# Four-layer gated cross-attention on one core: another order of the first loads, of the weight preparation and of VectorE's small work

## The chip, the cores and the metric

The kernel runs on one core of a Trainium2 chip. The metric is the device time of one execution in microseconds (us), the median of several runs. Everything is computed in float32. TensorE (PE) multiplies matrices, VectorE (DVE), ScalarE (ACT) and GpSimd (POOL) do the rest, and SyncE (SP) issues all transfers. A high-precision product is made from two parts of each operand, a rounded high part (ACT writes it) and the low part that is left (POOL or DVE subtracts), in three passes: high x high, high x low, low x high.

## What is computed

```python
# x, ctx: 8 blocks of 128 rows x 512.  LN = layer norm, g = gates
x = x + tanh(g_xattn[0]) * xattn0(LN(x), ctx)  # 32 heads of 128, position bias, mask; own residual
x = x + tanh(g_ffn[0])   * ffn0(LN(x))         # base + top-2 of 8 rank-16 experts
x = x + tanh(g_xattn[1]) * xattn1(LN(x), ctx)  # 16 query heads on 4 key heads of 96
x = x + tanh(g_ffn[1])   * ffn1(LN(x))         # as ffn0
x = x + tanh(g_xattn[2]) * xattn2(LN(x), ctx)  # one head of 512: softmax((x Wq+bq)(ctx Wk+bk)^T) ctx
x = x + tanh(g_ffn[2])   * ffn2(LN(x))         # w = (q - zero_point) * scale, by groups; x w^T + bias
x = x + tanh(g_xattn[3]) * xattn3(LN(x), ctx)  # 32 query heads of 16 on 8 key heads
x = x + tanh(g_ffn[3])   * ffn3(LN(x))         # activations rounded to -127..127 per row, gate/up/down
```

## The kernel before

Each engine has its own program, written out by hand in the order in which it shall run; semaphores join them. Rows go in blocks of 128 tokens, and from the second half-layer on in 4 pairs of blocks (`NPAIR`), inside which `j` is 0 or 1. `i` is the pair, `u` one of 8 units of a pair in the last attention.

**Prelude (first some 60 us).** SP issues the keys' weights of the first head pair (first chunk, then the rest), the transposed context in 4 chunks `c`, x in two halves of 4 blocks, the values' weights, the queries' weights and small tables (L388 to L404), all in one queue. ACT rounds chunk by chunk, DVE writes the context's low parts (L1737), POOL those of the weights (L526, L531). PE warms up with `BUSY` small products of the identity (L1122), then makes 4 key units chunk by chunk (L1131), and 8 value units (L1117). Between value units 1 to 5 it turns the blocks k and k+4 of x (`turn_x(k)`, L1145: a product with a diagonal matrix that also scales). For that DVE computes statistics of all 8 blocks (L1743 to L1754), POOL the powers (L537, L539), DVE applies them to 8 blocks (L1757), sums the query weights' blocks (`weight_sums`) and, for each k, multiplies what was turned by `ln_w` and forms sums (`rows_sums(k)`, L1766 to L1775) and later their low parts (`rows_low(k)`, L1780). `turn_x(k+1)` waits until `rows_sums(k)` has read the bank. POOL writes the low part of the first query weights (`split("q", 0)`, L520). The first query unit (L1098) waits for `x_split` and `wq_lo`.

**The head-pair loop** follows (some 80 to 810 us), then ffn0, xattn1 and ffn1. The change does not touch them.

**xattn2 (some 1304 to 1378 us).** Per pair PE runs `x2_pe(i)`: turn the next pair's rows (L1302), scores (L1485), first half of the next pair's keys (L1322), transpose the probabilities (L1493), second half of the keys, output (L1499), the next queries (L1322). DVE's `x2_dve(i)` takes row maxima (L2114), divides (L2118), writes low parts, statistics and keys, and updates x. Ahead of the first pair DVE dequantises ffn2's weights: 4 subtractions (L2371) and 4 multiplications (L2374) over 128x512 each. ACT rounds the result (`f2_weights`, before pair 2), POOL subtracts (L579). POOL also writes the context's low parts for the next pair (`context_rest`, L579), which the keys wait for (`cT_lo`).

**xattn3 (some 1408 to 1581 us)** works unit by unit: scores for unit U+2 (L1552), transposes of unit U (L1559), a filler product, then `attend(U)` (L1574). DVE's unit takes maxima and reciprocals and, after them, a slice of ffn3's preparation for the pair before (`first_pair`, `middle_pair`, `last_pair`): scales (L2143), rounding (`f3_round`, L2165), clipping (`f3_clip`, L2171). POOL divides the probabilities (L660) and multiplies (L652).

**ffn3 (the last 50 us)** per pair i: `f3_turn(i+1)`, `f3_gate_up(i+1, 0)`, transposes of pair i's inner rows (L1670), `f3_gate_up(i+1, 1)` (L1662), `f3_down(i)` (L1679). Before the very last transposes PE runs `BUSY_END` products of the identity (L1717).

## Time and profile before

| | |
|---|---|
| median of 3 runs | 1632.13 us (1632.02 to 1634.69) |
| profiled execution | 1633.68 us, its span 1632.0 us |
| TensorE clock granted, mean | 0.993 |
| busy: PE, DVE, ACT, POOL | 97%, 61%, 45%, 25% |
| PE not busy | 53.2 us of the span |

A busy share is an average over stages; the stages have different limits. Line numbers (L1131) are those of the kernel before. In a timeline, a row merges neighbouring instructions of one line: start, time from the first start to the last end, engine, line, what is written and read, how many, and in brackets the idle time of that engine ahead of it with what ended it.

### The profile page before, as it was taken

The numbers are of one execution on the slowest core, as the hardware profiler recorded it, in microseconds if no ns is written. First come the engines' busy times: TensorE is split into PE (matmuls) and PEld (weight loads), VectorE is DVE, ScalarE is ACT, GpSimd is POOL, SyncE is SP. The second block draws the span as 40 slices with busy tenths as digits, with TensorE's granted clock in tenths as the row PEclk, the third lists the DMA queues.
The fourth block names the chain that finished last, engine by engine and source line by source line (L and its number), as shares of the span: only waits on it lengthen the run. The fifth ranks groups of instructions, "written<-read, shape, count | busy, mean of one in ns | idle before, by whom it ended". The sixth has DMA issues, their size and how long they took to land.

```text
span 1632.0 us, 25948 instructions
## 1 busy us (share of the span) xinstructions
PE 1578.8 (97%) x8970; PEld 1267.8 (78%) x8970; DVE 989.5 (61%) x2627; ACT 741.7 (45%) x2149; POOL 403.5 (25%) x279
## 2 busy tenths in 40 slices
PE   8999999999999999999989999999999999899987
PEld 6788888888888888888875878778686787665556
DVE  6762663626636356363776674848475766756677
ACT  4442443424434244343432562726354322388863
POOL 3131320313203132031213300000001433376650
PEclk9999999999999999999999999999999999999999
DMA  5110111101111011110234000000001613000001
GB/s 177 53 43 30 56 42 51 42 29 55 42 51 42 29 55 42 51 42 29 78 88 184 14 1 13 0 13 0 0 1 41 219 52 106 14 14 14 1 1 52
DMA packets 34404, 76.22 MB, mean 47 GB/s; under 512 B 5537, under 2 KB 18465, under 8 KB 32161
## 3 DMA queue, kind: packets, MB, share of 16 engines
q1 hardware_dynamic: 34336, 75.36, 13.9%
q8 instruction: 38, 0.62, 0.2%
q14 instruction: 30, 0.24, 0.1%
HBM read 73.25 MB, written 2.10 MB: 46 GB/s over the span
## 4 chain that ended last, share of the span: by engine, by line
PE 79%; DVE 10%; ACT 5%; issue 3%; DVEq 2%; POOL 1%; DMA 1%; SPq 0%; POOLq 0%; ACTq 0%
PE banks L1172 11%; PE banks L1117 10%; PE banks L1090 9%; PE banks L1098 9%; PE banks L1322 9%; PE banks L1426 5%; PE banks L1228 3%; PE banks L1211 3%; PE banks L1398 3%; PE banks L1218 2%; PE banks L1529 2%; ACT p L967 1%; PE banks L1536 1%; PE banks L1552 1%; PE banks L1346 1%
## 5 line engine op out<-in xcount | busy, mean ns | idle before, releaser
L520 POOL TENSOR_TENSOR w_q<-w_raw_q,w_q 128x1792 fp32r<-128x1792 f32 x16 | 65.3, 4082 | 485.2 <-ACT w_q L727 485.2
L1172 PE MATMUL banks<-w_o,atT 128*128 128x512 f32 x720 | 180.2, 396 | 0.0
L1090 PE MATMUL banks<-cT,w_k 128*128 128x512 f32 x720 | 178.0, 396 | 0.0
L1117 PE MATMUL banks<-w_v,cT 128*128 128x512 f32 x768 | 177.3, 390 | 0.6 <-POOL w_v L531 0.4
L1117 PEld LDWEIGHTS banks<-w_v,cT 128*128 128x128 f32 x768 | 143.6, 188 | 31.6 <-POOL w_v L531 1.3
L1098 PE MATMUL banks<-xT,w_q 128*128 128x512 f32 x672 | 163.7, 394 | 0.7 <-ACT kT L717 0.7
L1841 DVE TENSOR_TENSOR sA<-banks,pbias 128x512 f32<-128x512 f32 x64 | 44.1, 690 | 186.4 <-PE banks L1211 185.7
L1172 PEld LDWEIGHTS banks<-w_o,atT 128*128 128x128 f32 x720 | 131.9, 188 | 25.7
L1090 PEld LDWEIGHTS banks<-cT,w_k 128*128 128x128 f32 x720 | 131.9, 188 | 25.6
L1098 PEld LDWEIGHTS banks<-xT,w_q 128*128 128x128 f32 x672 | 123.7, 188 | 26.0 <-ACT kT L717 1.1
L781 ACT ACTIVATE sA<-sA,nmA 128x128 f32<-128x128 f32 x256 | 99.5, 393 | 57.0 <-DVE nmA L1846 56.7
L1322 PE MATMUL banks<-xnT_part,wq 128*128 128x256 f32 x768 | 101.3, 285 | 0.0
L1868 DVE TENSOR_TENSOR x_res<-banks,x_res 128x512 f32<-128x512 f32 x112 | 77.1, 689 | 35.8 <-PE banks L1172 34.7
L717 ACT ACTIVATE vA<-banks 128x512 f32<-128x512 f32 x64 | 38.2, 597 | 131.0 <-PE banks L1117 130.9
L1322 PEld LDWEIGHTS banks<-xnT_part,wq 128*128 128x128 f32 x768 | 94.1, 190 | 2.2 <-issue 2.2
L967 ACT ACTIVATE p<-banks,nm 128x128 f32<-128x128 f32 x256 | 91.4, 407 | 8.7 <-DVE nm L2192 8.6
L891 ACT ACTIVATE p<-banks,nm 128x256 f32<-128x256 f32 x128 | 58.7, 484 | 68.0 <-DVE nm L2059 68.0
L787 ACT ACTIVATE pTA<-banks 128x512 f32<-128x512 f32 x64 | 38.1, 595 | 108.5 <-PE banks L1218 108.5
L1426 PE MATMUL banks<-wo,at 128*128 128x512 f32 x192 | 85.7, 592 | 0.0
L791 ACT ACTIVATE atT<-banks 128x512 fp32r<-128x512 f32 x64 | 38.3, 599 | 98.9 <-PE banks L1228 98.9
L1846 DVE CUSTOM_DVE_ANT_0 sA<-sA,madd 128x128 f32<-128x128 f32 x256 | 77.3, 357 | 8.8 <-issue 0.5
L660 POOL TENSOR_TENSOR p<-p,rs 128x512 f32<-128x512 f32 x64 | 67.9, 1066 | 41.3 <-DVE rs L2198 40.7
(280 smaller groups left out, 3246.4 us busy)
## 6 DMA issues: line engine op xcount, KB each, us to landing
w_raw_v<-in_w0v SPq DMA_DIRECT2D x8, 1024.0 KB, 4.8
w_raw_q<-in_w0q SPq DMA_DIRECT2D x16, 512.0 KB, 3.4
w_raw_k<-in_w0k SPq DMA_DIRECT2D x15, 512.0 KB, 3.5
w_raw_o<-in_w0o SPq DMA_DIRECT2D x15, 512.0 KB, 3.3
cTp<-in_ctxT SPq DMA_DIRECT2D x12, 512.0 KB, 3.9
wq_raw<-in_wq SPq DMA_DIRECT2D x1, 3072.0 KB, 10.2
wo<-in_wo SPq DMA_DIRECT2D x1, 3072.0 KB, 19.9
x_res<-in_x SPq DMA_DIRECT2D x2, 1024.0 KB, 10.9
```

What stands on the lines that cost most here:

```text
L520: pool.tensor_tensor(w_part[slot][1][:], w_raw[slot][:], w_part[slot][0][:].bitcast(F32), ALU.subtract).then_inc(S(f"w{slot}_lo"), 1)
L660: pool.tensor_tensor(p3[:, U % 3, k], p3[:, U % 3, k], rs[:, U % 3, k].unsqueeze(2).to_broadcast([P, 4, P]), ALU.mult).then_inc(S(f"x3_p{h ...
L781: e = act.activation(sA[:, g % 2, t, :], sA[:, g % 2, t, :], ACT.Exp, bias=nmA[:, g % 2, t:t + 1], scale=-1.0, accum_out=smA[:, g % 2, t:t ...
L967: e = act.activation(p3[:, U % 3, n, :], s[:, k, :], ACT.Exp, bias=nm[:, U % 3, n:n + 1], accum_out=sm[:, U % 3, n:n + 1])
L1090: mm = pe.matmul(dst, wk_[l][:, c, h * P:(h + 1) * P], cT[r][:, c, half * HT:(half + 1) * HT], start=c == 0 and n == 0, stop=c == DC - 1 a ...
L1098: mm = pe.matmul(dst, wq_[l][:, w, c, :], xT[r][:, x, c, :], start=c == 0 and n == 0, stop=c == 1 and n == len(PASSES) - 1)
L1117: mm = pe.matmul(dst, cT[l][:, c, b * P:(b + 1) * P], wv_[r][:, c, :], start=n == 0, stop=n == 3 * DC - 1)
L1172: mm = pe.matmul(dst, atT[l][:, h, t], w[r][:, h, :], start=n == 0, stop=n == 5)
L1322: mm = pe.matmul(dst, w(l, c), x(r, c), start=c == 0 and n == 0, stop=c == DC - 1 and n == len(PASSES) - 1)
L1426: mm = pe.matmul(bank(6 + b), at1[:, n, b * P:(b + 1) * P], wo1[:, n, :], start=n == 0, stop=n == NCH * KV1 - 1)
L1846: e = dve.tensor_tensor_reduce(out=sA[:, h, t, :], in0=sA[:, h, t, :], in1=madd[:, 4 * half + t, :], scale=-1.0, scalar=0.1 * BIG, op0=ALU ...
L1868: dve.tensor_tensor(x_res[:, b, :], bank(6 + b % 2), x_res[:, b, :], ALU.add).then_inc(S("o_added"), 1)
```

## The change

It reorders the first loads and cuts context chunk 1 in two for the rounding; it works the statistics by halves of 4 blocks; it moves the low part of the first query weights from POOL to DVE; it puts the dequantising for ffn2 between the pairs of xattn2, splits the keys there 3 to 1 around the transposes, moves one query product of xattn3 ahead of the first scores, moves slices of ffn3's preparation between units, moves one gate/up product ahead of a wait, and halves the last identity products. The rest of the arithmetic is as before.

```diff
-BUSY_END = 12
+BUSY_END = 6
-K_PARTS = (slice(0, 2 * P), slice(2 * P, DC * 2 * P))
+K_PARTS = (slice(0, 2 * P), slice(2 * P, 4 * P), slice(4 * P, DC * 2 * P))
+C_PARTS = [(c, slice(h * HT, (h + 1) * HT)) for c in range(2) for h in range(2)] + [(c, slice(0, NB * P)) for c in (2, 3)]
+X_ORDER = [b for k in range(NPAIR) for b in (k, k + NPAIR)]
...
# SyncE
-            sp.dma_start(w_raw["k"][:, K_PARTS[1]], A["w0k"][0][:, K_PARTS[1]]).then_inc(S("wk_ld"), 16)
-            for c in range(1, DC):
+            sp.dma_start(c_raw[:, 1, :], A["ctxT"][:, 1, :]).then_inc(S("c1_loaded"), 16)
+            k_rest = slice(K_PARTS[1].start, K_PARTS[2].stop)
+            sp.dma_start(w_raw["k"][:, k_rest], A["w0k"][0][:, k_rest]).then_inc(S("wk_ld"), 16)
+            for c in range(2, DC):
                 sp.dma_start(c_raw[:, c, :], A["ctxT"][:, c, :]).then_inc(S(f"c{c}_loaded"), 16)
-            for k in range(2):
-                sp.dma_start(x_res[:, 4 * k:4 * k + 4, :], x_dram[:, 4 * k:4 * k + 4, :]).then_inc(S(f"x{k}_loaded"), 16)
             load("v", A["w0v"][0])
+            for n in range(2):
+                for b in (2 * n, NPAIR + 2 * n):
+                    sp.dma_start(x_res[:, b:b + 2, :], x_dram[:, b:b + 2, :]).then_inc(S(f"x{n}_loaded"), 16)
             load("q", A["w0q"][0])
...
# GpSimd
-            pool.wait_ge(S("a_var"), 1)
-            pool.tensor_tensor(rstd[:], ve[:], neg_half[:], ALU.pow).then_inc(S("a_rstd"), 1)
-            pool.wait_ge(S("a_var"), 2)
-            pool.tensor_tensor(rr[:], ms[:], neg_half[:], ALU.pow).then_inc(S("a_rstd"), 1)
-            pool.wait_ge(S("xr_ready"), NB)
-            split("q", 0)
+            for n in range(2):
+                t = slice(n * NPAIR, (n + 1) * NPAIR)
+                pool.wait_ge(S("a_var"), n + 1)
+                pool.tensor_tensor(xrs[:, :, t], xvar[:, :, t], neg_half[:, 0:NPAIR].unsqueeze(1).to_broadcast([P, 2, NPAIR]),
+                                   ALU.pow).then_inc(S("a_rstd"), 1)
             split("k", 1)
...
# ScalarE: context by C_PARTS, the keys' weights in three parts
+            store_v(0, bank(0), K_UNITS + 1)
             act.wait_ge(S("const_ready"), 1)
-            act.wait_ge(S("a_rstd"), 2)
-            diagonal(0)
-            store_v(0, bank(0), K_UNITS + 1)
-            for k in range(1, NPAIR):
+            for k in range(NPAIR):
+                if k % 2 == 0:
+                    act.wait_ge(S("a_rstd"), k // 2 + 1)
                 diagonal(k)
-            store_v(1, bank(1), K_UNITS + 2)
-            round_q(0)
+                if k == 1:
+                    store_v(1, bank(1), K_UNITS + 2)
             for b in range(2, NB):
                 store_v(b, bank(b % 2), K_UNITS + b + 1)
                 if b < 2 + NPAIR:
                     rows_high(b - 2)
+                if b == 2:
+                    round_q(0)
...
# TensorE
-                pe.wait_ge(S("c_lo"), c + 2 if c else 1)
-                for n, u in enumerate((0, 2, 1, 3) if c == 0 else range(4)):
+                pe.wait_ge(S("c_lo"), 2 * c + 1 if c < 2 else c + 3)
+                for n, u in enumerate((0, 2, 1, 3) if c < 2 else range(4)):
...
                 if not last:
-                    x2_keys(i + 1, 0)
+                    x2_keys(i + 1, range(DC - 1))
                 for j in range(2):
                     pe.wait_ge(S("x2_p"), 2 * i + j + 1)
                     pe.transpose(bank(2 + j)[:, 0:P], p2[:, j, :], ident[:]).then_inc(S("x2_tp"), 1)
                 if not last:
-                    x2_keys(i + 1, 1)
+                    x2_keys(i + 1, (DC - 1,))
...
                 pe.wait_ge(S("kv3_ready"), 4)
+                x3_queries(0, 2, 3, 6)
                 scores(0)
                 scores(1)
-                x3_queries(0, 2, G3, 6)
+                x3_queries(0, 3, G3, 6)
...
                 f3_gate_up(i + 1, 0)
+                if i == 0:
+                    f3_gate_up(i + 1, 1)
                 f3_turn_inner(i, 0)
                 f3_turn_inner(i, 1)
-                f3_gate_up(i + 1, 1)
+                if i > 0:
+                    f3_gate_up(i + 1, 1)
...
# VectorE, first layer (the statistics, their scales and their use are now
# functions of a half n; x_stats, x_scales and x_apply each take 4 blocks)
+            x_stats(0)
+            x_scales(0)
+            x_stats(1)
+            x_apply(0)
+            x_scales(1)
             dve.wait_ge(S("g_loaded"), 64)
...
-            for k in range(NPAIR):
-                rows_sums(k)
-                if k >= 1:
-                    rows_low(k - 1)
+            rows_sums(0)
+            x_apply(1)
+            weight_sums(0)
+            rows_sums(1)
+            rows_low(0)
+            dve.wait_ge(S("wq_hi"), 1)
+            dve.tensor_tensor(w_part["q"][1][:], w_raw["q"][:], w_part["q"][0][:].bitcast(F32),
+                              ALU.subtract).then_inc(S("wq_lo"), 1)
+            rows_sums(2)
+            rows_low(1)
+            rows_sums(3)
+            rows_low(2)
             rows_low(NPAIR - 1, 0, 0, 2)
             rows_low(NPAIR - 1, 1, 2, 7)
...
# VectorE, fourth layer, middle_pair
+                    if u == 2 and i + 2 < NPAIR:
+                        ln_stats(2 * i + 4)
                     if u == 2 and i > 1:
                         f3_scales(i - 2)
                         f3_round(i - 2)
                     if u == 3:
                         f3_apply(i - 1)
-                        if i + 2 < NPAIR:
-                            ln_stats(2 * i + 4)
# last_pair
                     if u == 0:
                         f3_max(i - 2, 1, 1)
+                        f3_scales(i - 2)
                     if u == 1:
                         updated(i - 1, 1)
-                        f3_scales(i - 2)
+                        f3_round(i - 2, (0,))
                     if u == 2:
                         ln_stats(2 * i - 2, 2, "f3_var")
-                        f3_round(i - 2)
                     if u == 3:
+                        f3_round(i - 2, (1,))
                         f3_apply(i - 1)
-                    if u == 4:
-                        f3_clip(i - 2)
...
                 updated(NPAIR - 1, 0)
-                f3_clip(NPAIR - 2)
+                f3_clip(NPAIR - 3)
                 updated(NPAIR - 1, 1)
...
             ln_stats(NB - 2, 2, "f3_var")
+            f3_clip(NPAIR - 2, (0,))
             f3_apply(NPAIR - 1)
...
             inner_clip()
+            f3_clip(NPAIR - 2, (1,))
             f3_max(NPAIR - 1, 0, 1)
...
# VectorE, third layer (layer index 2)
-            dve.wait_ge(S("f2_ld"), 16 * (1 + 4 * DC))
-            for c in range(DC):
-                dve.tensor_tensor(zp2[:, c, :], w2q[:, c, :], zp2[:, c, :], ALU.subtract)
-            dve.drain()
-            for c in range(DC):
-                dve.tensor_tensor(zp2[:, c, :], zp2[:, c, :], sc2[:, c, :], ALU.mult)
-            dve.drain().then_inc(S("scaled"), 1)
+            (the same two loops are now f2_offsets() and f2_scales())
             next_stats(0)
             next_apply(L2X, 0)
             x2_keys(0)
-            pairs_split(dve, x2_dve, nothing, nothing, nothing)
+            x2_dve(0, False)
+            f2_offsets()
+            x2_dve(1, False)
+            f2_scales()
+            x2_dve(2, False)
+            x2_dve(3, True)
```

## Rows read from the trace of the kernel before

**Rows 1.** The page's busy times.

```profile
PE 1578.8 (97%) x8970; PEld 1267.8 (78%) x8970; DVE 989.5 (61%) x2627; ACT 741.7 (45%) x2149; POOL 403.5 (25%) x279
```

**Rows 2.** PE's waits over the span: us in total, times, longest.

```profile
PE banks L1670 <- DVE iq L2348: 6.3, 4, 3.2
```

**Rows 3.** Timeline, start and arrival of loads (start, us, engine, line).

```profile
11.75 10.04 PE L1131 MATMUL banks<-cT,w_k 128*128 128x512 f32 x36 [2.12 <-DVE cT L1737]
...
14.06 2.47 DVE L1743 BATCH_NORM_STATS2 stat<-x_res 128x6 f32<-128x512 f32 x4 [0.18 <-DMA x_res<-in_x]
...
19.25 2.19 ACT L713 ACTIVATE w_v<-w_raw_v 128x512 fp32r<-128x512 f32 x4 [6.84 <-DMA w_raw_v<-in_w0v]
```

**Rows 4.** Timeline, the rows of x in the prelude.

```profile
29.07 2.05 PE L1145 MATMUL banks<-diag,x_res 128*128 128x128 f32 x16 [0.31 <-ACT diag L757]
...
33.95 4.22 POOL L520 TENSOR_TENSOR w_q<-w_raw_q,w_q 128x1792 fp32r<-128x1792 f32 x1 [5.73 <-ACT w_q L727]
34.20 4.25 DVE L1773 TENSOR_TENSOR stage_q<-stage_q 128x256 f32<-128x256 f32 x1
...
47.34 2.02 DVE L1780 TENSOR_TENSOR xT<-stage_o,xT 128x1792 fp32r<-128x1792 f32 x1
...
55.18 5.18 PE L1098 MATMUL banks<-xT,w_q 128*128 128x512 f32 x22
```

**Rows 5.** Busy times by window; behind POOL's the granted clock.

```profile
14.00:16.00 2.00, 2.00 (x6) 1.54 (x5) 1.94 (x4) 0.00 (x0) 0.00 (x0) 0.50 1.09 410
...
1322.00:1324.00 2.00, 2.00 (x10) 2.00 (x11) 0.00 (x0) 0.00 (x0) 0.00 (x0) 0.50 0.49 133
```

**Rows 6.** Timeline, start of xattn2; last row: the second pair's keys.

```profile
1306.39 6.48 DVE L2371 TENSOR_TENSOR zp<-w2q,zp 128x512 f32<-128x512 int32 x4
...
1318.17 3.14 POOL L579 TENSOR_TENSOR cT_part<-cTp,cT_part 128x256 fp32r<-128x256 f32 x4
...
1319.23 0.66 PE L1302 MATMUL banks<-ident,xn 128*128 128x128 f32 x4 [2.68 <-DVE xn L1829]
...
1321.84 3.78 PE L1485 MATMUL banks<-k,q 128*128 128x128 f32 x16 [0.63 <-DVE k L2108]
1325.27 3.72 PE L1322 MATMUL banks<-cT_part,wk 128*128 128x256 f32 x24
...
1341.63 3.08 PE L1322 MATMUL banks<-cT_part,wk 128*128 128x256 f32 x24
```

**Rows 7.** Timeline, xattn2's later pairs.

```profile
1339.93 1.95 PE L1485 MATMUL banks<-k,q 128*128 128x128 f32 x16
...
1341.47 0.29 DVE L2114 TENSOR_REDUCE nm<-banks 128x1 f32<-128x128 f32 x1 [5.85 <-PE banks L1485]
...
1361.59 0.33 PE L1493 MATMUL banks<-ident,p 128*128 128x128 f32 x1 [0.89 <-DVE p L2118]
```

**Rows 8.** Timeline, PE in xattn3: first scores, and keys in pair 1.

```profile
1416.55 1.99 PE L1552 MATMUL banks<-kbd,q 64*128 64x512 f32 x8 [1.08 <-ACT q L958]
...
1487.04 1.99 PE L1514 MATMUL banks<-cTp,wk 128*128 128x256 f32 x8 [1.20 <-DVE y L2202]
```

**Rows 9.** Timeline, last pair of xattn3.

```profile
1559.64 2.45 DVE L2165 TENSOR_SCALAR qs<-xs,rsc 128x512 f32<-128x512 f32 x4
...
1568.37 4.10 DVE L2171 TENSOR_SCALAR qs<-qs 128x512 f32<-128x512 f32 x4
...
1574.33 0.65 PE L1559 MATMUL banks<-ident,p 128*128 128x128 f32 x4 [1.09 <-POOL p L660]
```

**Rows 10.** Timeline, ffn3.

```profile
1596.58 1.12 PE L1670 MATMUL banks<-ident,iq 128*128 128x128 f32 x4 [3.21 <-DVE iq L2348]
1597.35 3.28 PE L1662 MATMUL banks<-wg,qTs 128*128 128x256 f32 x16
...
1601.17 0.48 DVE L2329 SCALAR_TENSOR_TENSOR sg<-banks,xsc,eg 128x256 f32<-128x256 f32 x1 [1.51 <-ACT eg L1007]
...
1623.86 2.84 PE L1717 MATMUL banks<-ident 128*128 128x128 f32 x24
```

More of the change, by code:

```diff
@@ L185, in build @@
         rv = sb(ctx_a, "rv", [P, NB])
[L186 to L187 removed]
+        xvar = sb(ctx_a, "xvar", [P, 2, NB])
+        xrs = sb(ctx_a, "xrs", [P, 2, NB])
         ctx_a.close()
@@ L732, in _ @@
                 context_chunk(0, slice(half * HT, (half + 1) * HT), "ab"[half])
+            for c, t in C_PARTS[2:4]:
+                context_chunk(c, t)
             act.wait_ge(S("wk_ld"), 16)
             round_part("k", K_PARTS[1])
-            for c in range(1, DC):
-                context_chunk(c)
+            round_part("k", K_PARTS[2])
+            for c, t in C_PARTS[4:]:
+                context_chunk(c, t)
             act.wait_ge(S("wv_ld"), 16)
@@ L1460, in x1_pe, with x2_product @@
                 project(1, NCH * (KV1 - 1), NCH * KV1)
-            def x2_product(w, t, b0, done, halves=(0, 1)):
-                for oc in range(DC // 2 * halves[0], DC // 2 * (halves[-1] + 1)):
+            def x2_product(w, t, b0, done, chunks=range(DC)):
+                for oc in chunks:
                     mm = split_product(bank(b0 + oc // 2)[:, (oc % 2) * PT2:(oc % 2 + 1) * PT2],
@@ L1691, in _ @@
             pe.wait_ge(S("res"), NB * L2X)
-            x2_keys(0, 0)
-            x2_keys(0, 1)
+            x2_keys(0, range(DC))
             pairs_ahead(pe, x2_pe)
@@ L1733, in weight_sums @@
                 dve.tensor_tensor(w[:, WS4], w[:, W12], w[:, WS2], ALU.subtract).then_inc(S("q_sum"), 1)
-            for n, (c, t) in enumerate([(0, slice(0, HT)), (0, slice(HT, NB * P))] + [(c, slice(0, NB * P)) for c in range(1, DC)]):
+            for n, (c, t) in enumerate(C_PARTS):
                 dve.wait_ge(S("c_hi"), n + 1)
@@ L1759, in _, with x_stats, x_scales @@
-            weight_sums(0)
+            def x_stats(n):
+                dve.wait_ge(S(f"x{n}_loaded"), 32)
+                for k in range(n * NPAIR, (n + 1) * NPAIR):
+                    dve.bn_stats(stat[:, k, :], x_res[:, X_ORDER[k], :])
+            def x_scales(n):
+                t = slice(n * NPAIR, (n + 1) * NPAIR)
+                dve.drain()
+                for k in range(n * NPAIR, (n + 1) * NPAIR):
+                    dve.bn_aggr(mv[:, k, :], stat[:, k, :])
+                dve.drain()
+                dve.tensor_scalar(xvar[:, 0, t], mv[:, t, 1], EPS, None, ALU.add)
+                dve.drain()
+                dve.reciprocal(rv[:, t], xvar[:, 0, t])
+                dve.drain()
+                dve.tensor_tensor(xvar[:, 1, t], mv[:, t, 1], rv[:, t], ALU.mult)
+                dve.drain()
+                dve.tensor_scalar(xvar[:, 1, t], xvar[:, 1, t], EPS, None, ALU.add).then_inc(S("a_var"), 1)
@@ L1760, in _, with x_apply @@
+            def x_apply(n):
+                dve.wait_ge(S("a_rstd"), n + 1)
+                for k in range(n * NPAIR, (n + 1) * NPAIR):
+                    b = X_ORDER[k]
+                    dve.tensor_scalar(x_res[:, b, :], x_res[:, b, :], mv[:, k, 0:1], xrs[:, 0, k:k + 1], ALU.subtract,
+                                      ALU.mult).then_inc(S("xr_ready"), 1)
+            x_stats(0)
[3 more added lines that the diff above has]
+            x_scales(1)
             dve.wait_ge(S("g_loaded"), 64)
@@ L2160, in f3_scales, with f3_round @@
                 scales(xsc[:, i], rsc[:], am[:])
-            def f3_round(i):
-                for j in range(2):
+            def f3_round(i, js=(0, 1)):
+                for j in js:
                     for w in range(2):
```

46 lines of the change are left out of this document (17 added, 29 removed).

## The prediction, made before the changed kernel was run

> **What bounds the kernel now.** I read the page's busy times first: PE is busy for 1578.8 us of the 1632.0 us span, so all its waiting is 53.2 us [rows 1]. Then PE's waits, first in total and then stretch by stretch. The head-pair loop (80 to 800 us) shows none, the change does not touch it, and ffn0, xattn1 and ffn1 keep theirs. So the sum is made of waits at four places: the prelude, the start of xattn2, xattn3 and ffn3, where the largest wait sits (L1670, 6.3 us in 4 times) [rows 2]. Third the windows with the granted clock. Some waits are followed by PE at half clock (0.50, the level of 1.2 GHz) [rows 5]: such a wait costs twice, once as idle time and once in slower matmuls.
>
> **Prelude.** PE waits 2.12 us for context chunk 1 at 11.75, then the 36 matmuls take 10.04 us, with the clock at 0.50 from 14 to 16 [rows 3, 5]. At full clock a value unit's 12 matmuls follow each other every 2.8 us, so the 36 would take 8.4. Now chunk 1 comes before the rest of the keys' weights and is split by halves. DVE can finish it by 9.8 and POOL its weights by 10.2, so PE would begin some 1.5 us earlier and, if the clock stays up, end its keys 3.2 us earlier, at 18.6. The values' weights no longer wait behind x. x's first megabyte is usable at 14.06 and the values' weights, the second megabyte after it, at 19.25 [rows 3]: 2.6 us each. So the weights arrive at about 14.1, x's halves at 16.7 and 19.2, and both value units can be done at 24.1. After that the chain is DVE's. From the rows: statistics of 4 blocks take 2.47 [rows 3], and I take 1.4 for scales, 1.7 for POOL's power, 1.9 to apply 4 blocks, 3.1 for a `rows_sums`, 1.8 for the weight sums and 2.02 for a low part of 128x1792 [rows 4]. In the new order that makes statistics to 19.3, scales to 21.0 (POOL is still on the values), statistics to 23.5, apply to 25.4. The first turn of x is then at 24.5, against 29.07 [rows 4].
>
> From there PE has 24 us of work up to the queries, but DVE has more. The query weights' low part moves onto it (+2.0). What goes is a stall: POOL's 4.22 us at 33.95 covers DVE's L1773, which takes 4.25 us for 128x256 [rows 4], where its neighbours take 0.43, so 3.8 us come back. Adding the list up, the sums of k=2 come at 41.2, the last turn waits about 2.3 us for them, and DVE gives the first queries' rows free at 51.4 with PE done at 51.8. Queries began at 55.18 [rows 4]: 3.4 us. That new wait may bring a short half clock, worth up to 1.7. I take 3.0; bounds 0 (DVE eats it all) and 5.
>
> The Trainium skill (SBUF — State Buffer, Who interferes with whom) says that VectorE and GpSimd take a shared port pair in turns, and that the second to come stands still for the whole of the other's instruction. The L1773 row agrees. By it a DVE instruction moved into a time when POOL works can cost POOL's length. The place to fear it here is the dequantising, the second rival.
>
> **Start of xattn2.** DVE's subtractions take 6.48 us and push the turned rows back: PE waits 2.68 us before L1302 at 1319.23, then 0.63, and then runs the scores in 3.78 us instead of 1.95, at clock 0.50 [rows 5 to 7]. With both dequantising steps gone from there, the statistics run at 1306.4, and the rows are ready near 1312.3, after POOL's low parts. PE finishes the first keys at 1316.55 and turns x at once. DVE's last two key copies (0.8) let the scores start at 1317.65, not 1321.84. But a wait takes part of the place. The next keys need the context's low part, for which ACT copies only after 1316.55 (1.1 us) and POOL takes 3.1 [rows 6]: 1320.8. The scores end at 1319.4, so PE waits about 1.4 us that was hidden before. The keys start at 1320.8 instead of 1325.27 [rows 6], 4.5 us, and their 24 matmuls take the 3.08 of later pairs, not 3.72 [rows 6]: 5.1 in all. Bounds: 3 (the clock falls again) and 6.8 (no such wait).
>
> The subtractions now stand behind pair 0's updates, the multiplications behind pair 1's. In each pair DVE has an empty 5.85 us there [rows 7]. Free of POOL the steps take 0.68 and 0.62 us an instruction, 2.7 and 2.5 in all. POOL's context parts may cost 1.3 more, so each fits, and nothing is added. ACT's rounding before pair 2 finds its input a microsecond or so early.
>
> **Keys 3 to 1.** At pair 2 ACT and POOL prepare ffn2's weights, the probabilities come late, and PE waits 0.89 for the second block and 0.18 before the first [rows 7]. One key chunk is worth 1.46 us, so the longer cover hides both: 1.1 us. After the transposes 1.46 us of keys remain, more than the 0.9 that ACT's copies need. In pairs 0 and 1 nothing waited, so nothing changes.
>
> **xattn3.** The query product moved ahead (1.8 us) fills the 1.08 us wait [rows 8] but starts the scores 0.6 us later. ACT and not PE then sets the pace, and it gets its second queries 0.3 us earlier: 0.3 (0 to 1.1). In pair 1 PE waits 1.20 us for the copy of y [rows 8], and straight ahead of the copy stand 1.7 us of statistics. A unit earlier they delay a row maximum by 0.5 that has 0.9 to spare: 1.2. In the last pair the 2.45 us of rounding is split in two and the 4.10 us of clipping leaves the loop [rows 9]. After the clipping PE waited 1.09 for POOL [rows 9] and 0.70 for ACT. The maximum behind it can come 2.7 us earlier, but ACT's copies and POOL's queue give back only 1.0 to 1.5. The half of the rounding before the copy of y eats what the other half saves there, so the 1.38 us wait and the half clock near 1566 stay. I take 1.3 (0.5 to 4, the upper end if that wait and its half clock go too).
>
> **ffn3.** The 3.21 us wait [rows 10] takes in the gate/up product, 2.15 us of PE at full clock, which took 3.28 after it. But DVE's chain sets the end. It can use an earlier sigmoid: at 1601.17 it had waited 1.51 [rows 10]. Against that it now carries half a clipping (0.7) there, so 0.8. The other half falls into 0.82 us in which DVE waited for POOL's power. At the end the 12 identity products take 2.84 us from 1623.86 and reach 1626.4 [rows 10], while the inner rows were ready at 1625.5. Half of them, 1.4 us, ends before that: 0.9.
>
> **Sum.** 3.0 + 5.1 + 1.1 + 0.3 + 1.2 + 1.3 + 0.8 + 0.9 = 13.7 us. The profiled execution took 1633.68 us, 1.55 more than the median, and would come to 1620.0; from the median 1632.13 it is **1618.4 us**. With every part at its lower end 7.5 us remain, 1624.6; with every part at its upper end it is 20.9, 1611.2.
>
> **Rivals.**
> *The prelude gives nothing* (0.15). Moving the low part makes DVE the bound of the rows of x. For it: DVE is at work almost without a break from 27 to 56 us. Against: the 3.8 us stall goes for 2.0 us of work. Time: 1632.1 - 10.7 = 1621.4.
> *The dequantising collides with POOL in the attention* (0.04), the case on the other side. The four subtractions took 6.48 us beside POOL [rows 6]; three of them ran in 0.6, so one stood for some 4.6. If all eight instructions did, a group would take 18.5 us in a gap of 5.85 [rows 7]: 12.7 late, twice, with some 2.4 at half clock after each. Time: 1632.1 - 13.7 + 25.4 + 4.8 = 1648.6. It decides from the point where a group takes more than the gap and has eaten the 13.7, that is from about 11 us a group. Against it: POOL has one block of 3.1 us there [rows 6], not a row of them.
> *More than I see comes back* (0.17). The clock stays up through the last pair and the last turn of x, and the context's low part is in time: 6 us more, 1612.5.
> *The waits go but others fill in* (0.06), because DVE is in every chain: only xattn2's statistics and the identity products count, 1626.
> *The forecast itself* has 0.58.
>
> **How the numbers follow.** The likeliest case gives 1618.4. The range 1612.5 to 1624.0 takes in the first and most of the third rival and leaves out some 0.15. What a measurement can tell from no change is 0.2%, 3.3 us. Faster by more is all but the second rival and the tail of the fourth: 0.93; within it 0.03; slower 0.04.
>
> **What would show it.** Prelude: L1131's second group starts near 10.2 and its clock stays up; queries start near 52; the L1773 row is 0.43; the last turn of x waits 2 us. xattn2: no wait of L1302, a new wait of L1322 for POOL's context part of about 1.4, L2371 about 2.7 to 4 after the first pair. xattn3: no wait for y in pair 1; no L2171 inside the last pair. ffn3: the first L1670 wait about 1.1 and the last row of identity products half as long. A span above 1625, or the queries after 54, would prove me wrong in the prelude; keys of pair 1 after 1322, counted with the prelude's shift, in xattn2.

## The result, and the profile after

| | before | after |
|---|---|---|
| median, runs of the first comparison | 1632.86 us (4 runs, 1632.02 to 1634.69) | 1619.04 us (4 runs, 1618.59 to 1620.08) |
| ratio, 95% interval | | 0.9915 (0.9898 to 0.9932) |
| median, second comparison | 1631.89 us (11 runs, 1629.27 to 1637.60) | 1618.80 us (5 runs, 1617.55 to 1622.02) |
| ratio, 95% interval | | 0.9918 (0.9901 to 0.9935) |
| profiled execution, its span | 1633.68, 1632.0 us | 1619.05, 1617.3 us |

The change takes 13.1 to 13.8 us off the median; 13.7 were forecast from the profiled execution. The two profiled spans differ by 14.7 us. The rows of after, one fence for each view, with the group of before that each answers to. The page's busy times [rows 1] and PE's waits in total [rows 2]:

```profile
PE 1572.8 (97%) x8958; PEld 1264.1 (78%) x8958; DVE 981.2 (61%) x2633; ACT 742.1 (46%) x2151; POOL 399.3 (25%) x278
...
PE banks L1682 <- DVE iq L2380: 4.8, 4, 1.6
```

The prelude of after, timeline [rows 3, 4]:

```profile
7.33 11.49 PE L1142 MATMUL banks<-cT,w_k 128*128 128x512 f32 x48
...
14.02 2.20 ACT L719 ACTIVATE w_v<-w_raw_v 128x512 fp32r<-128x512 f32 x4 [1.47 <-DMA w_raw_v<-in_w0v]
...
16.74 2.47 DVE L1757 BATCH_NORM_STATS2 stat<-x_res 128x6 f32<-128x512 f32 x4 [2.84 <-DMA x_res<-in_x]
...
24.09 1.95 PE L1156 MATMUL banks<-diag,x_res 128*128 128x128 f32 x16
...
35.02 0.42 DVE L1798 TENSOR_TENSOR stage_o<-stage_o 128x256 f32<-128x256 f32 x1
...
37.79 2.02 DVE L1814 TENSOR_TENSOR w_q<-w_raw_q,w_q 128x1792 fp32r<-128x1792 f32 x1
...
40.55 2.02 PE L1156 MATMUL banks<-diag,x_res 128*128 128x128 f32 x16 [2.17 <-DVE stage_a L1791]
```

All 48 key products run without a wait; the small instruction that took 4.25 us takes 0.42; the last turn of x waits 2.17 us (2.3 forecast). The queries begin at 50.61, against 55.18. Then xattn2, timeline [rows 6, 7]:

```profile
1314.11 2.05 PE L1496 MATMUL banks<-k,q 128*128 128x128 f32 x16 [0.27 <-DVE k L2141]
...
1316.97 4.35 PE L1333 MATMUL banks<-cT_part,wk 128*128 128x256 f32 x36 [0.81 <-POOL cT_part L585]
...
1322.76 1.88 PE L1510 MATMUL banks<-ctk,pT 128*128 128x512 f32 x4
...
1326.42 3.02 DVE L2404 TENSOR_TENSOR zp<-w2q,zp 128x512 f32<-128x512 int32 x4
1332.54 0.29 DVE L2147 TENSOR_REDUCE nm<-banks 128x1 f32<-128x128 f32 x1 [3.10 <-PE banks L1496]
...
1352.95 0.38 PE L1504 MATMUL banks<-ident,p 128*128 128x128 f32 x2
```

PE's wait for the turned rows is gone, there is a new one of 0.81 for the context's low part (1.4 forecast), four subtractions in 3.02 us with 3.10 idle behind them, and no wait for probabilities at pair 2. xattn3 and ffn3, timeline of PE [rows 8 to 10]:

```profile
1413.05 1.13 PE L1563 MATMUL banks<-kbd,q 64*128 64x512 f32 x4 [1.66 <-ACT q L969]
...
1553.59 1.48 PE L1540 MATMUL banks<-wo,y 128*128 128x512 f32 x2 [1.53 <-DVE y L2235]
...
1562.97 0.91 PE L1585 MATMUL banks<-pT,vbd 128*32 128x128 f32 x16 [0.70 <-ACT pT L985]
...
1577.78 4.06 PE L1674 MATMUL banks<-wg,qTs 128*128 128x256 f32 x32 [0.55 <-DVE sg L2365]
1583.16 0.66 PE L1682 MATMUL banks<-ident,iq 128*128 128x128 f32 x4 [1.32 <-DVE iq L2380]
```

Windows with the granted clock behind POOL's busy time [rows 5]:

```profile
14.00:16.00 2.00, 2.00 (x11) 1.65 (x10) 0.00 (x0) 1.98 (x4) 1.27 (x2) 1.00 1.05 397
...
1322.00:1324.00 2.00, 2.00 (x12) 1.33 (x11) 1.04 (x3) 0.96 (x1) 0.00 (x0) 1.00 0.00 0
1554.00:1556.00 2.00, 2.00 (x18) 0.60 (x16) 0.97 (x4) 1.83 (x11) 2.00 (x2) 0.56 0.00 0
...
1586.00:1588.00 2.00, 2.00 (x8) 1.60 (x8) 1.66 (x6) 1.45 (x3) 0.00 (x0) 0.50 0.00 0
```

The half clock is gone at 14 and at 1322. In this execution it stays behind the wait for y, and in ffn3 it has moved to the product behind the transposes. One more difference was in no step of the forecast: in ffn1's last pair, whose code is unchanged, PE of after waited 1.21 us for `hs` (the experts' inner rows, which VectorE writes and PE transposes) and PE of before did not. So one question of the experiments was how much of a pair of profiles holds for the runs.

### The profile page after: what moved, and what is told of

Its sections match the earlier page's. It is cut to its first block, busy times and chain, and to the rows that moved or that the text cites. A ratio compares the mean times of both kernels' runs of the same rounds, so it can differ in the third digit from the quotient of the medians.

```text
span 1617.3 us, 25912 instructions
## 1 busy us (share of the span) xinstructions
PE 1572.8 (97%) x8958; PEld 1264.1 (78%) x8958; DVE 981.2 (61%) x2633; ACT 742.1 (46%) x2151; POOL 399.3 (25%) x278
## 4 chain that ended last, share of the span: by engine, by line
PE 78%; DVE 10%; ACT 5%; issue 3%; DVEq 2%; POOL 1%; DMA 1%; POOLq 0%; SPq 0%; ACTq 0%
PE banks L1183 11%; PE banks L1128 10%; PE banks L1101 9%; PE banks L1109 9%; PE banks L1333 9%; PE banks L1437 5%; PE banks L1239 4%; PE banks L1222 3%; PE banks L1409 3%; ACT p L978 2%; PE banks L1229 2%; PE banks L1540 2%; PE banks L1563 1%; PE banks L1357 1%; PE banks L1547 1%
## 5 line engine op out<-in xcount | busy, mean ns | idle before, releaser
L527 POOL TENSOR_TENSOR w_q<-w_raw_q,w_q 128x1792 fp32r<-128x1792 f32 x15 | 61.1, 4070 | 479.6 <-ACT w_q L733 479.6
L585 POOL TENSOR_TENSOR cT_part<-cTp,cT_part 128x256 fp32r<-128x256 f32 x32 | 23.3, 765 | 228.5 <-ACT cT_part L858 228.5
```

The costliest lines, as they stand in the source:

```text
L527: pool.tensor_tensor(w_part[slot][1][:], w_raw[slot][:], w_part[slot][0][:].bitcast(F32), ALU.subtract).then_inc(S(f"w{slot}_lo"), 1)
```

## The experiments

Twelve further sets of runs followed, in three groups of four; each group shares its runs of before (medians 1632.46, 1631.89 and 1631.43 us). Each kernel left one profile.

### The parts, each alone on the kernel before

**Prelude alone** (`a1_prelude`): all edits of the change up to the head-pair loop.

```diff
+ C_PARTS, K_PARTS in three, loads in the new order, x_stats/x_scales/x_apply by halves
-            split("q", 0)                      # GpSimd
+            dve.tensor_tensor(w_part["q"][1][:], w_raw["q"][:], ...)   # VectorE, behind rows_low(0)
```

> The kernel before with the prelude's part of the change alone (order of the loads, context chunk 1 by halves, statistics by halves, the first query weights' low part on VectorE). Theory from the two traces: the first queries start 4.6 us earlier than before, near 50.6, and this carries through the untouched middle; the time falls by 4.6 us, or by 3.4 if the one small VectorE instruction in ffn1's last pair (L1855 after the change, 1.67 us instead of 0.38) again stands for a whole POOL instruction. The forecast said 3.0. Rival, the prelude gives nothing because VectorE becomes the bound: within 1 us of before. If the ffn1 stall is chance, this profile or one of the next three lacks it; if it hangs on the prelude's shift, it is here and in none of the runs without the prelude.

Measured: 1628.85 us (11 runs, 1627.24 to 1633.18), ratio 0.9980 (0.9971 to 0.9989), 3.6 us less by medians. But its profiled execution was a long one (1631.15), and its queries started at 54.61, only 0.6 earlier. Its timeline of PE, the products of chunk 1 and the last turn of x:

```profile
11.87 10.07 PE L1142 MATMUL banks<-cT,w_k 128*128 128x512 f32 x36 [1.83 <-POOL w_k L533]
...
42.92 3.55 PE L1156 MATMUL banks<-diag,x_res 128*128 128x128 f32 x16 [1.92 <-DVE stage_a L1788]
```

The first load landed 0.55 us later than in after (ACT rounds it at 3.78, not 3.23), context chunk 1 was rounded at 9.28 and not 7.73, so PE waited 1.83, and the clock stood at 0.61 and 0.54 from 12 to 16. The `hs` wait was there as well (1.22). The 4.0 us between this start of the queries and after's are, by the rows, three parts: x's first half was usable 1.31 us later (VectorE's statistics start at 18.05, not 16.74), PE's late keys held up VectorE's sums by 1.05, and the last turn was followed by half clock, 1.6 more (`c_loads`, below). The gain is real and varies. The rival that the `hs` wait hangs on the prelude falls with `a3_x3` and `a4_end`, which have the wait without this prelude.

**Dequantising alone** (`a2_dequant`).

```diff
-            (subtractions and multiplications)   next_stats(0) ... pairs_split(dve, x2_dve, ...)
+            x2_dve(0, False); f2_offsets(); x2_dve(1, False); f2_scales(); x2_dve(2, False); x2_dve(3, True)
```

> The kernel before with only the dequantising moved into xattn2's attention. Theory: the second keys start some 5 us earlier although nothing else has changed, and the 5.85 us gaps of VectorE hide the two steps (about 3.0 us each): time lower by 5.1 to 5.7 us. Rival, collision with POOL in the gaps: a step takes over 5 us and the gain falls under 3 us. Rival, the gain needs the three to one split of the keys: the waits for the probabilities at pair 2 grow and under 4 us remain.

Measured: 1629.76 us (11 runs, 1628.58 to 1631.62), ratio 0.9985 (0.9976 to 0.9994), 2.7 us less by medians: a miss, although its profile shows the whole 5.5 us in its place (output of pair 0 at 1326.33, against 1331.88) and neither rival: the two groups took 3.02 and 2.95 us, and only 0.4 us was lost from there to xattn3's keys. The next two profiles suggest a reason.

**xattn3's part alone** (`a3_x3`).

```diff
+                x3_queries(0, 2, 3, 6)      # ahead of scores(0), scores(1)
+                    ln_stats(2 * i + 4) in unit 2; last pair: scales in unit 0, rounding in units 1 and 3, no clipping
```

> The kernel before with only xattn3's part: one query product ahead of the first scores, and VectorE's statistics, rounding and clipping moved between units. The forecast's terms give 0.3 + 1.2 + 1.3 = 2.8 us less; by the two traces it is 0.4 + 1.15 + 2.4 = 4.0 us less. Rival, the moved clipping comes back at the start of ffn3 (its half there is paid for in full): under 2 us less.

Measured: 1627.62 us (6 runs, 1626.97 to 1628.10), ratio 0.9966 (0.9954 to 0.9978), 4.8 us less by medians; the rival falls. From xattn3's first keys to the last down product it took 216.0 us, against 219.5 in before: 3.5. Its course through the untouched ffn1 and xattn2 differs from the profile of before, though (timeline, all engines):

```profile
1297.44 1.65 DVE L1823 TENSOR_SCALAR ve<-mv 128x2 f32<-128x2 f32 x1
...
1302.43 0.53 PE L1349 MATMUL banks<-ident,hs 128*128 128x128 f32 x2 [1.20 <-DVE hs L2007]
...
1307.29 5.29 DVE L2371 TENSOR_TENSOR zp<-w2q,zp 128x512 f32<-128x512 int32 x4
1308.55 4.62 POOL L579 TENSOR_TENSOR cT_part<-cTp,cT_part 128x256 fp32r<-128x256 f32 x4
...
1321.12 2.05 PE L1485 MATMUL banks<-k,q 128*128 128x128 f32 x16 [1.03 <-DVE k L2109]
```

A VectorE instruction on two numbers per row takes 1.65 us, PE waits 1.20 for `hs`; then VectorE's subtractions take 5.29 and not 6.48 us, GpSimd's context part stands still instead (4.62, not 2.86), and the scores run in 2.05, not in 3.78 at half clock.

**ffn3's part alone** (`a4_end`).

```diff
+                if i == 0: f3_gate_up(i + 1, 1)      # ahead of the transposes
-BUSY_END = 12
+BUSY_END = 6
```

> The kernel before with only ffn3's part: the second gate/up product of pair 1 ahead of pair 0's transposes, and 6 identity products at the end instead of 12. Forecast 0.8 + 0.9 = 1.7 us less, by the two traces about 1.5 us less. Rival, the half clock only moves from the gate/up product to the product behind it and VectorE's chain sets the end: 0.9 us less, the identity products alone.

Measured: 1630.28 us (11 runs, 1628.65 to 1630.88), ratio 0.9984 (0.9975 to 0.9993), 2.2 us less; by its profile 2.6 us from xattn3's first keys on. The second transposes of inner rows follow the first after 8.98 us:

```profile
1595.07 0.66 PE L1670 MATMUL banks<-ident,iq 128*128 128x128 f32 x4 [1.32 <-DVE iq L2351]
...
1604.05 0.66 PE L1670 MATMUL banks<-ident,iq 128*128 128x128 f32 x4 [1.13 <-DVE iq L2351]
```

In before it was 10.59 (10.10 to 11.07 in the three other profiles with ffn3 as in before), in after 10.33. So the gate/up product is worth more by itself (1.6 us) than in the whole change, where VectorE carries a clipping in that stretch.

### On the changed kernel

**The changed kernel again** (`b0_after`), no edit.

> The changed kernel itself, once more, beside more runs of before. The four single parts summed to 13.3 us of medians without the keys' split. Theory: 13.3 + 1.1 for the keys, less some 1.3 that ffn3 gives back when the clipping stands in VectorE's chain there, so about 13 us under before. Two places of a profile should differ from execution to execution: the prelude (the second group of key products either follows without a wait at full clock and the queries start near 50.6, or the first loads land about 1.3 us later, PE waits some 1.8 us and runs at half clock, and the queries start up to 4 us later), and ffn1's last pair (a 1.2 us wait for hs, or none). Rival: those two are fixed properties of the changed kernel, and this profile repeats the first one in both.

Measured: see the table on top; 13.1 us under before, as expected. In its profile chunk 1's products waited 0.85 us, the queries started at 51.76, and the `hs` wait was there (1.21). The first place varies as expected; the second showed the `hs` wait in every profile with this prelude, and only `c_poolq` (below), which changes the prelude, lacks it.

**Keys 2 to 2 again** (`b1_keys22`).

```diff
-                    x2_keys(i + 1, range(DC - 1))
+                    x2_keys(i + 1, range(DC // 2))
```

> The changed kernel with xattn2's keys split 2 to 2 around the transposes again. Theory: PE waits 0.9 us for the second block's probabilities at pair 2 and 0.2 before the first, output of pair 2 comes 1.1 to 1.2 us later, and the time is 1.1 us above the changed kernel. Rival, the three to one split costs each pair something (pairs took 15.91 us after and 15.72 in the profile of before): the loop's period falls to 15.72 and only 0.7 us are lost. Against it: with the dequantising alone moved, at 2 to 2, the period was 15.92 too.

Measured: 1621.39 us (6 runs, 1618.88 to 1624.09), ratio 0.9931 (0.9915 to 0.9947), 2.6 us above the changed kernel by medians, an interval that holds 0 and the 1.1. The profile gives the size: the wait is back,

```profile
1354.52 0.33 PE L1504 MATMUL banks<-ident,p 128*128 128x128 f32 x1 [0.89 <-DVE p L2151]
```

and from pair 0's output to xattn3's keys it takes 76.66 us, against 74.93 to 75.49 in the seven profiles at 3 to 1: 1.2 to 1.7. The wait itself is worth 1.2: from pair 1's output to pair 2's it takes 17.09 us, against 15.91 in after. The rival falls: the first period is 15.92 and did not shrink.

**Clipping beside the wait** (`b2_clip`).

```diff
                 f3_clip(NPAIR - 3)
+                f3_clip(NPAIR - 2)
                 updated(NPAIR - 1, 1)
...
-            f3_clip(NPAIR - 2, (0,))   # and (1,), both in ffn3
```

> The changed kernel with pair 2's clipping taken out of VectorE's chain in ffn3 and put where VectorE waits 1.90 us for the last but one output of xattn3, as in the kernel before, behind pair 1's clipping. Theory: ffn3's second transposes of inner rows follow the first after 9.0 us, as they did with ffn3's part alone, and not after 10.3; the 0.7 before the first are saved too: 1.3 to 2.0 us under the changed kernel. Rival, a half clock in ffn3 or ScalarE sets the end there: under 0.5 us.

Measured: 1617.97 us (4 runs, 1616.74 to 1619.43), ratio 0.9912 (0.9893 to 0.9931); 0.8 us under the changed kernel, not settled by these runs. The profile shows the step at 9.34 us, not 9.0:

```profile
1582.51 0.66 PE L1682 MATMUL banks<-ident,iq 128*128 128x128 f32 x4 [1.33 <-DVE iq L2381]
...
1591.85 0.66 PE L1682 MATMUL banks<-ident,iq 128*128 128x128 f32 x4 [1.48 <-DVE iq L2381]
```

From xattn3's keys to the end 1.1 us are saved (212.1, against 213.2 in `b0_after`), a little under the 1.3 expected.

**And the last pair's rounding behind y** (`b3_clip_last`), on top of `b2_clip`.

```diff
                     if u == 3:
-                        f3_round(i - 2, (1,)); f3_apply(i - 1)
+                        f3_apply(i - 1, (0,))
+                    if u == 4:
+                        f3_round(i - 2, (1,)); f3_apply(i - 1, (1,))
```

> As the one before, and in the last pair of xattn3 the second half of the rounding and of the normalisation stand behind the copy of y, a unit later. Theory: y is copied 1.7 us earlier, PE's 1.53 us wait for it goes, and the half clock that follows (1554 to 1558) goes with it: 1.5 to 3 us more. Rival, the moved instructions meet GpSimd's row of multiplications in that unit and stand for them, the row maxima come late: nothing gained, or up to 2 us lost, to be seen as long instances of the rounding or the normalisation.

Measured: 1617.28 us (4 runs, 1615.10 to 1618.93), ratio 0.9902 (0.9883 to 0.9922). The stage from xattn3's keys to the end is 212.07 us, as without it (212.11): nothing gained, as the rival had it. Timeline of PE:

```profile
1554.20 1.12 PE L1540 MATMUL banks<-wo,y 128*128 128x512 f32 x2 [0.23 <-DVE y L2235]
...
1558.14 0.66 PE L1570 MATMUL banks<-ident,p 128*128 128x128 f32 x4 [0.52 <-POOL p L666]
...
1561.12 0.66 PE L1570 MATMUL banks<-ident,p 128*128 128x128 f32 x4 [0.90 <-POOL p L666]
1562.12 0.66 PE L1570 MATMUL banks<-ident,p 128*128 128x128 f32 x4 [0.34 <-POOL p L666]
```

1.30 us of the wait for y go. In their place stand 2.1 us of waits for GpSimd's divisions (the three shown and one more of 0.34), where `b2_clip` has 0.53, and two roundings took 1.87 us where they had taken 1.22. `b2_clip` had no half clock behind its wait for y, so this pair does not test whether the half clock goes with the wait.

**Chunk 1's weights first** (`c_loads`).

```diff
+            sp.dma_start(w_raw["k"][:, K_PARTS[1]], ...)   # 128 KB, then the context chunk
             sp.dma_start(c_raw[:, 1, :], ...)
-            sp.dma_start(w_raw["k"][:, k_rest], ...)       # 384 KB
+            sp.dma_start(w_raw["k"][:, K_PARTS[2]], ...)   # 256 KB
```

> The changed kernel with the keys' weights for chunk 1 (128 KB) loaded and rounded ahead of context chunk 1, and the weights of chunks 2 and 3 (256 KB) behind it, instead of all 384 KB behind it. In four of five profiles since, PE waited 0.8 to 1.8 us before chunk 1's products, each time for the low part of these weights, and the queries started at 51.2 to 54.6 instead of 50.6. Theory: that wait goes in this profile, the queries start at 50.5 to 51.5, and the median is 1 to 2 us under the changed kernel. Rival, the context chunk's own low part becomes the last: a wait of about 0.5 stays and the gain is under 0.5 us.

Measured: 1619.92 us (5 runs, 1617.66 to 1621.09), ratio 0.9923 (0.9910 to 0.9936): nothing gained (the changed kernel had 0.9918). The wait at chunk 1 is gone in its profile, and the queries still start at 52.55. One part of the cause is when x lands (timeline of DVE, then of PE):

```profile
17.05 2.47 DVE L1758 BATCH_NORM_STATS2 stat<-x_res 128x6 f32<-128x512 f32 x4 [2.92 <-DMA x_res<-in_x]
...
40.87 2.83 PE L1157 MATMUL banks<-diag,x_res 128*128 128x128 f32 x16 [2.14 <-DVE stage_a L1792]
```

The last turn starts 23.82 us after VectorE's first statistics. In after, `b0_after`, `b1_keys22`, `b2_clip`, `b3_clip_last` and `c_best` it is 23.81 to 23.83, with x usable anywhere from 16.74 to 17.89. The other part stands behind the last turn, in the granted clock of this window, of this kernel:

```profile
42.00:44.00 2.00, 2.00 (x11) 1.90 (x10) 1.93 (x4) 0.79 (x1) 0.00 (x0) 0.50 0.03 8
```

and of the profiled execution of after:

```profile
42.00:44.00 2.00, 2.00 (x13) 1.74 (x12) 1.93 (x4) 1.10 (x1) 0.00 (x0) 1.00 0.04 8
```

In seven profiles with this wait at 2.13 to 2.17 us the queries start 10.04 to 10.06 us after the last turn (four) or 11.66 to 11.68 after it (three, each with the half clock). `a1_prelude`, with a wait of 1.92, took 11.69. So x's landing and the chain of VectorE behind it set that turn, and not the wait at chunk 1, as long as that is short; in `a1_prelude`, where it was 1.83 with half clock behind it, PE came late to the first turn and the last one stood 24.87 us after the first statistics.

**Low part on GpSimd again** (`c_poolq`).

```diff
+            split("q", 0)     # GpSimd, behind its second power
-            dve.tensor_tensor(w_part["q"][1][:], ...)
```

> The changed kernel with the low part of the first query weights on GpSimd again. Theory: one small instruction of VectorE (128x256, 0.42 us) stands for GpSimd's 4.2 us again, the sums of k=1 or k=2 come some 2 us later net (3.8 more, 2.0 less), and the queries and the end are 1 to 2 us later. Rival, GpSimd's instruction now falls where VectorE does not need the shared path: the same time, or 2 us less because VectorE has 2.0 less to do.

Measured: 1622.43 us (5 runs, 1621.18 to 1623.46; a sixth took 5417 us, at a granted clock of 0.28, for a reason that nothing here shows), ratio 0.9940 (0.9928 to 0.9953), 3.6 us above the changed kernel by medians, more than expected. Timeline, all engines:

```profile
35.49 4.30 POOL L527 TENSOR_TENSOR w_q<-w_raw_q,w_q 128x1792 fp32r<-128x1792 f32 x1 [6.67 <-ACT w_q L734]
35.81 4.26 DVE L1799 TENSOR_TENSOR stage_o<-stage_o 128x256 f32<-128x256 f32 x1
...
43.26 3.75 PE L1157 MATMUL banks<-diag,x_res 128*128 128x128 f32 x16 [4.05 <-DVE stage_a L1792]
```

The stall is back as before, PE waits 4.05 instead of 2.14: the last turn comes 25.73 us after the first statistics, 1.9 later, and the half clock (0.50 from 42 to 48) adds 2.4. The queries start at 55.76, after before's 55.18: without this one move the new prelude gives nothing. The runs agree, 3.6 us lost here against the 3.6 that `a1_prelude` gained. The move alone on the kernel before was not run.

**Three edits together** (`c_best`): `b2_clip`, `c_loads`, and in ffn1 GpSimd's power ahead of its additions.

```diff
-                    add_bias(L, i, t); rsqrt(...)
+                    rsqrt(...); add_bias(L, i, t)      # in ffn1
```

> The changed kernel with three things: the clipping beside the wait (1.0 us measured in its profile), the keys' weights of chunk 1 first, and in ffn1 GpSimd's power for the next pair ahead of its two additions. Theory of the third: VectorE's tiny instruction (L1855) no longer meets GpSimd's additions, takes under 0.4 and not 1.67 us, and PE's wait of 1.2 us for hs in the last pair, seen in 6 of 6 profiles with the changed prelude, goes. Together 3 to 4 us under the changed kernel, about 1615. Rival, the additions now meet another VectorE instruction of the same chain and the 1.2 us stays: 2 to 2.5 us.

Measured: 1622.73 us (5 runs, 1620.82 to 1625.24), ratio 0.9948 (0.9935 to 0.9961): 3.9 us above the changed kernel by medians. The theory of the third edit fell. Timeline, all engines:

```profile
1297.43 2.56 POOL L568 TENSOR_TENSOR xb<-x_res,tb_f 128x512 f32<-128x512 f32 x2
...
1299.14 0.87 DVE L2032 TENSOR_TENSOR tw<-tw,e 128x2 f32<-128x2 f32 x1
...
1301.64 0.52 PE L1363 MATMUL banks<-ident,hs 128*128 128x128 f32 x2 [1.33 <-DVE hs L2042]
```

The instruction of L1855 (L1858 here) takes 0.17 us now, but the additions meet the next tiny instruction of the chain (0.87 for 0.16), and in three pairs, not in one. A pair of ffn1 takes 12.18 us for 10.81. By itself the third edit costs 4.3 us on the kernel before (next), which is about all that is lost here: the other two edits show no gain in these runs.

**The third edit on the kernel before** (`d_before_order`).

```diff
-                    add_bias(L, i, t); rsqrt(...)
+                    rsqrt(...); add_bias(L, i, t)      # in ffn1
```

> The kernel before with only that third edit. The profiles of before's order at the start of xattn2 show two courses: without the wait for hs, VectorE's subtractions take 6.48 us, PE waits 2.68 and then runs at half clock, and the output of pair 0 comes 36.2 us after the last pair's base product of ffn1; with the wait (1.2 us), the subtractions take 5.3 us, GpSimd's context part stands instead, and the output comes after 33.3 to 33.7. Theory: taking the 1.2 us wait away puts the kernel on the first course and makes it up to 2 us slower, no faster. Rival, the stall is a plain loss: 1.2 us faster.

Measured: 1635.72 us (10 runs, 1634.24 to 1636.55), ratio 1.0023 (1.0014 to 1.0032), 4.3 us slower. It is slower as the theory said, but not by its mechanism: the `hs` wait did not go, it came in three pairs (1.33 to 1.36 each). So this run does not decide what taking the wait away is worth.

### The fourteen profiles side by side

Worked out from PE's rows, in us: the queries' start; PE's wait for `hs` in ffn1's last pair; from that pair's first base product to pair 0's output in xattn2; from there to xattn3's first keys; from there to the start of the last down product.

| profile | queries | hs | to output | to keys | to end |
|---|---|---|---|---|---|
| before | 55.18 | 0 | 36.23 | 76.02 | 219.49 |
| a2_dequant | 55.28 | 0 | 30.69 | 76.38 | 219.58 |
| a3_x3 | 55.20 | 1.20 | 33.70 | 76.40 | 216.01 |
| a4_end | 55.25 | 1.19 | 33.33 | 76.38 | 216.90 |
| a1_prelude | 54.61 | 1.22 | 33.72 | 76.40 | 219.83 |
| d_before_order | 55.03 | 1.35 | 33.70 | 76.38 | 219.49 |
| after | 50.61 | 1.21 | 31.59 | 75.49 | 214.13 |
| b0_after | 51.76 | 1.21 | 31.81 | 74.93 | 213.23 |
| b1_keys22 | 52.75 | 1.21 | 31.60 | 76.66 | 214.05 |
| b2_clip | 51.21 | 1.23 | 31.59 | 75.49 | 212.11 |
| b3_clip_last | 52.69 | 1.21 | 31.58 | 75.45 | 212.07 |
| c_loads | 52.55 | 1.21 | 31.74 | 75.46 | 213.24 |
| c_poolq | 55.76 | 0 | 30.70 | 75.11 | 213.93 |
| c_best | 50.73 | 1.33 | 32.08 | 75.49 | 212.01 |

## Why the prediction was right, and where it was right by luck

The total and the side came out; the terms only partly, and two errors of opposite sign cancelled in part.

**Prelude (3.0 forecast).** Right in mechanism and in size. In six profiles with exactly this prelude the queries start at 50.6 to 54.6, at 52.3 on average, against 55.2: 2.9 us. The single pair of profiled executions says 4.6, the medians of `a1_prelude` 3.6. What I had as a footnote, "that new wait may bring a short half clock, worth up to 1.7", is one part of the scatter: 1.6 us, in four of eight profiles. Another is when x lands, 16.74 to 18.05, which I took as fixed at 16.7 from one profile. By my own sign of being wrong (queries after 54) the profile of `a1_prelude`, at 54.61, would have counted against me, though its median is 3.6 us lower. The claim that the low part's move frees a 3.8 us stall for 2.0 of work is the core of it (`c_poolq`).

**Start of xattn2 (5.1 forecast).** A step that failed, as a size. Against the profiled execution it is 4.6 (36.23 to 31.59), or 5.5 where neither has the `hs` wait. But the course that I priced, with 6.48 us of subtractions and a half clock behind them [rows 5, 6], is one of two; it stands in one of five profiles that dequantise ahead of xattn2. In that one VectorE's first subtraction stood still while all four of GpSimd's instructions ran:

```profile
1306.39 4.68 DVE L2371 TENSOR_TENSOR zp<-w2q,zp 128x512 f32<-128x512 int32 x1
```

In the other four the two engines took turns, one instruction each (some 1.2 us for 0.7 on both sides), the scores ran in 2.05 us without a half clock, and the stretch takes 33.3 to 33.7, with the `hs` wait of 1.2 to 1.35 in it. Against those the move is worth 1.7 to 2.1, and `a2_dequant`'s runs say 2.7 (1.0 to 3.9). That most executions of before take the cheaper course is what this suggests; no run shows how often each comes. The 1.4 us wait that I expected for the context part measured 0.81.

The Trainium skill (SBUF — State Buffer, Who interferes with whom) says that the order of issue decides which of the two engines blocks. The traces agree that one engine stands still for the whole of the other's instruction, and the same two rows went both ways in executions of the same code (6.48 and 2.86 us in before, 5.29 and 4.62 in `a3_x3`). But the order of the starts does not tell the two apart here: VectorE's first subtraction starts 1.27 us ahead of GpSimd's first of the four in before and 1.26 ahead in `a3_x3`. I priced one outcome alone.

**The collision (second rival, 0.04).** Rightly small: the two moved groups took 3.02 and 2.95 us in their gap and delayed nothing.

**Keys (1.1).** Right: the wait at pair 2 is worth 1.2 in `b1_keys22`.

**xattn3 and ffn3 (0.3 + 1.2 + 1.3 + 0.8 + 0.9 = 4.5).** Measured 5.4 to 6.3 from xattn3's keys to the end, in the five profiles that have this part as in the change. The first two terms were right (0.4 and 1.15 in the profiles).

The last pair was under-sized: 2.4 in after, not 1.3. Behind the copy of y 1.2 came back, inside the 1.0 to 1.5 of the forecast. The step that failed is the one ahead of it: "the half of the rounding before the copy of y eats what the other half saves there". The 1.38 wait for y did stay (1.53), but 2 us ahead of it PE waited for GpSimd's division, a wait that the forecast does not price. That division waits for VectorE, whose row maximum stood behind the whole 2.45 us of rounding [rows 9]. The row of before, then that of after:

```profile
1563.95 0.66 PE L1559 MATMUL banks<-ident,p 128*128 128x128 f32 x4 [1.43 <-POOL p L660]
...
1551.40 0.66 PE L1570 MATMUL banks<-ident,p 128*128 128x128 f32 x4 [0.30 <-POOL p L666]
```

So y's product comes 1.2 us earlier. The 1.09 wait of rows 9 is no part of the gain: it is missing in `a1_prelude`, `a2_dequant` and `a4_end` too, where nothing of xattn3 was changed and the stage took as long. The spread from 5.4 to 6.3 is a half clock behind the wait for y: it costs 0.9 and stood in `a3_x3`, after, `b1_keys22` and `c_poolq`, and not in `b0_after`, `b2_clip`, `c_loads` and `c_best`, with the same wait of 1.53.

ffn3's two terms measured 2.6 by themselves and 1.4 in the change, where 1.7 were forecast; the identity products gave 1.0 in both. I charged half a clipping at 0.7. It holds up VectorE's chain by 0.86, and VectorE then idles 0.66 us ahead of the update of x where it idled 0.17 in `a4_end`: together the 1.35 between the steps of 8.98 and 10.33. What ends that idle time is not shown. The half clock behind the down product in after has no part in it: `b0_after` has none there and the same step (10.34).

**Sum.** By averages over the profiles: 2.9 for the prelude, 2 to 2.6 for xattn2's start, 1.0 for the keys, 5.8 from xattn3 on, 11.7 to 12.3 us. The runs say 13.1 and 13.8, with intervals of 10.6 to 16.6, and the medians of the four parts add up to 13.3. Forecast 3.0 + 5.1 + 1.1 + 4.5 = 13.7. The excess in xattn2 (2.5 to 3) and the shortfall behind it (1.3) cancel in part; the averages are of few profiles and fall 1 to 2 us short of the runs. That the total came out within 1 us is closer than its terms were, and so partly luck.

What stays open: what starts the `hs` wait. Of the twelve profiles whose ffn1 is as in before it stood in nine. In the three without it VectorE's tiny instruction got its turn between GpSimd's two additions. When it came does not tell them apart: 0.98, 0.98 and 0.94 us after the start of the additions in before, `a2_dequant` and `c_poolq`, where it took 0.38 to 0.40, and 0.92 to 0.95 in the nine others, where it took 1.65 to 1.69. Nor is it the prelude: `a3_x3` and `a4_end` run the same code as before up to there. The two edits that should beat the changed kernel are not proven to: `b2_clip` and `b3_clip_last` are 0.8 and 1.5 us under it with overlapping intervals; the first one's 1.1 us in its stage is shown by the profile alone.

## What to carry to other kernels

One profiled execution is one draw: before a stall or a half clock is priced, look whether its row is the same in a second profile, and where two engines exclude each other price both orders. A wait that goes on one engine comes back as another's where several engines run close behind each other: count what the next one in line has to spare. Find the one load that the chain hangs on before reordering others: here the start of the queries followed x's landing at a fixed distance, and the loads of the keys did not move it. And look first for a small instruction that takes ten times its neighbours: with the long one that it stands behind put back on GpSimd, the rest of the new prelude gained nothing.

## What the runs showed of the hardware

- VectorE and GpSimd hold each other up in both directions. A 128x256 VectorE instruction of 0.42 us took 4.26 beside one of 4.30 us on GpSimd (`c_poolq`). One VectorE subtraction took 4.68 us, over four GpSimd instructions of 0.77 (before). An instruction on 128x2 elements took 1.65 to 1.69, over a second GpSimd addition of 1.3. GpSimd's four 128x256 instructions took 4.62 us for 2.86 beside VectorE's subtractions (`a3_x3`).
- The same wait of 2.13 to 2.17 us on PE was followed by half clock (0.50) for some 3 us in three executions and by none in four, and the same wait of 1.53 by half clock in four and by none in four.
- The loads of the first 20 us land at different times in executions of the same code: context chunk 1 was rounded at 7.73 in after and at 9.28 in `a1_prelude`, and x's first half was usable at 16.74 and at 18.05.
